# Tokenizer loop: the token products with stationary and moving operand traded, two tokens side by side in the array, and two elementwise products on GpSimd

## What is computed

```
Ct = B[None] * C / (1.0 - dtA / 2) * dt[:, None]      # C is x
dA = (1.0 + dtA / 2) / (1.0 - dtA / 2)
dA_log = jnp.log(dA)
V = jnp.exp(dA_log[:, :, None] * l)                   # l = 0 .. 511
K = 2.0 * jnp.einsum('chn,hnl->chl', Ct, V).real      # c: 16 elements, h: 256 tokens, n: 64 states
```

## Time and profile before

| | |
|---|---|
| three runs | 1660.93, 1664.78, 1665.66 us (median 1664.78) |
| the profiled execution | 1662.74 us, of which the span is 1661.0 us |
| TensorE, weight loads, VectorE, ScalarE, GpSimd busy | 89%, 59%, 77%, 60%, 35% of the span |
| TensorE's granted clock, mean | 0.906 of 2.4 GHz |
| loop of the tokens | first matmul at 80.23 us, last copy from PSUM over at 222.1 us |

### The profile page before, as it was taken

One profiled execution on the slowest core, in us unless ns is written; L12 is line 12 of the kernel. 1 busy time (PEld: TensorE's weight loads), 2 busy tenths in 40 slices (PEclk: granted clock), 3 DMA queues, 4 the chain that ended last, 5 costly groups with the idle time before them and its releaser, 6 DMA issues. The chain is left out here.

```text
span 1661.0 us, 31577 instructions
## 1 busy us (share of the span) xinstructions
PE 1473.0 (89%) x11710; PEld 986.5 (59%) x11710; DVE 1272.4 (77%) x2389; ACT 1002.0 (60%) x2539; POOL 580.4 (35%) x600
## 2 busy tenths in 40 slices
PE   2099967999999999999978888789999599999997
PEld 2099955677766777667756766567665244444443
DVE  8999926777777777777753346269998599999996
ACT  7799916887888877888752224178885233333331
POOL 0000004545445544454530000027777433333332
PEclk9555558999999999999988699989999899999998
DMA  2022252332333233332245037177785244444443
GB/s 83 1 51 64 61 151 84 100 101 94 104 125 102 94 95 105 116 103 98 94 161 178 0 116 241 47 217 206 214 221 137 52 103 101 101 101 102 102 102 83
DMA packets 233098, 183.09 MB, mean 110 GB/s; under 512 B 163568, under 2 KB 164976, under 8 KB 232944
## 3 DMA queue, kind: packets, MB, share of 16 engines
q1 hardware_dynamic: 232944, 181.07, 38.1%
HBM read 93.98 MB, written 59.77 MB: 93 GB/s over the span
## 5 line engine op out<-in xcount | busy, mean ns | idle before, releaser
L1063 PE MATMUL al_ps<-w,al_xT 128*128 128x512 f32 (+2 forms) x1024 | 351.3, 497 | 0.0
L1063 PEld LDWEIGHTS al_ps<-w,al_xT 128*128 128x128 f32 x1024 | 192.2, 193 | 127.1 <-issue 107.3
L2221 POOL TENSOR_TENSOR ff_zq<-ff_z,ff_back 128x1024 bf16<-128x1024 fp8e4 x64 | 122.6, 1915 | 222.9 <-DVE ff_z L2245 222.9
L451 PE MATMUL tk_ps<-tk_w,tk_l 128*128 128x64 f32 x512 | 119.6, 422 | 57.7 <-DVE tk_w L420 50.8
L2187 ACT ACTIVATE ff_sg<-af_ps 128x1024 f32<-128x1024 f32 x64 | 65.5, 1024 | 150.7 <-PE af_ps L2270 150.7
L451 PEld LDWEIGHTS tk_ps<-tk_w,tk_l 128*128 128x128 f32 x512 | 114.2, 332 | 60.3 <-issue 60.3
L756 POOL TENSOR_TENSOR al_qv<-al_qv,al_qe 128x512 f32<-128x512 f32 x48 | 63.2, 1316 | 219.8 <-PE al_ps L1126 219.8
L2270 PE MATMUL af_ps<-wgT,xqT 128*128 128x512 bf16 x512 | 122.7, 383 | 13.6 <-ACT ff_sg L2187 13.6
L2291 PE MATMUL af_ps<-wdT,ff_zT 128*128 128x512 bf16 x512 | 123.9, 386 | 5.9 <-DMA ff_zT<-ff_zq 5.9
L2270 PE MATMUL af_ps<-wuT,xqT 128*128 128x512 bf16 x512 | 122.1, 381 | 6.8 <-DVE ff_z L2237 4.8
L2042 PE MATMUL af_ps<-ag_w,ag_aT 128*128 128x512 f32 x256 | 112.6, 593 | 1.7 <-ACT af_ps L1878 1.7
(11 more groups left out here) (299 smaller groups left out, 3388.8 us busy)
## 6 DMA issues: line engine op xcount, KB each, us to landing
al_hx<-h_s SPq DMA_DIRECT2D x36, 256.0 KB, 2.7
o_s<-al_o SPq DMA_DIRECT2D x32, 272.0 KB, 2.2
h_s<-tk_w SPq DMA_DIRECT2D x16, 512.0 KB, 3.8
v_s<-al_v SPq DMA_DIRECT2D x32, 256.0 KB, 2.3
k_s<-al_kT SPq DMA_DIRECT2D x32, 256.0 KB, 2.3
q_s<-al_qT SPq DMA_DIRECT2D x32, 256.0 KB, 2.7
lt_k<-k_s SPq DMA_DIRECT2D x16, 512.0 KB, 5.0
lt_v<-v_s SPq DMA_DIRECT2D x16, 512.0 KB, 3.7
```

Of the source, the lines that this page charges most:

```text
L451: ins = pe.matmul(o, L[:, u, 0, t], R[:, u, t], start=True, stop=t < CS)
L1063: ins = pe.matmul(out, xT[:, T, k], w[:, k, cols], start=False, stop=True, skip_group_check=True)
L2221: pool.tensor_tensor(zq[:, u].rearrange("p (k s) -> p k s", s=QB), z8[:, u].rearrange("p (k s) -> p k s", s=QB), back[:, u, :, None].to_br ...
```

## The change

L is no longer summed: both k go to TensorE for all 16 tokens. The operands trade places. R(t), 64 columns, is now stationary, and L(k, t), 128 columns, moving. The 64 x 128 result of an even token goes to partitions 0 to 63 of PSUM and that of the odd one to 64 to 127, with the two alternating in program order. The result of a pair is a transposed one, so ScalarE copies it to `mid` (`turned`), TensorE transposes it (`turns`, 8 for a chunk, one chunk late), and ScalarE copies that to `hs` (`tokens`). R's product and the multiplication a · frequency go to GpSimd; ScalarE adds the offset in one instruction for the chunk.

```diff
@@ scalar
             def phases(ch):
-                if ch >= 2:
-                    act.wait_ge(nf_ready, ch - 1)
-                for t in range(CH):
-                    ins = act.activation(ph[:, ch % 2, t], c("iota_a"), ACT.Identity,
-                                         scale=par[:, 1, ch * CH + t:ch * CH + t + 1], bias=c("off_r"))
-                ins.then_inc(ph_ready, 1)
+                act.wait_ge(raw_ready, ch + 1)
+                act.activation(ph[:, ch % 2], ph[:, ch % 2], ACT.Identity, bias=c("off_r")).then_inc(ph_ready, 1)
...
+            def turned(ch):
+                act.wait_ge(mm_ready, ch + 1)
+                if ch >= 2:
+                    act.wait_ge(tr_ready, ch - 1)
+                for k in range(2):
+                    ins = act.activation(mid[:, ch % 2, 4 * k:4 * k + 4], ps[ch % 2 * 2 + k][:].rearrange(
+                        "p (j q) -> p j q", j=4), ACT.Copy)
+                ins.then_inc(mid_ready, 1)
+
             def tokens(ch):
-                act.wait_ge(mm_ready, ch + 1)
+                act.wait_ge(tr_ready, ch + 1)
...
                 if ch:
-                    tokens(ch - 1)
+                    turned(ch - 1)
+                if ch >= 2:
+                    tokens(ch - 2)
+            tokens(NCH - 2)
+            turned(NCH - 1)
             tokens(NCH - 1)
+
+        @block.gpsimd
+        def _(pool):
+            def raw(ch):
+                if ch >= 2:
+                    pool.wait_ge(nf_ready, ch - 1)
+                t0 = ch * CH
+                pool.tensor_tensor(ph[:, ch % 2], par[:, 1, t0:t0 + CH, None].to_broadcast([P, CH, 64]),
+                                   c("iota_a")[:, None, :].to_broadcast([P, CH, 64]), ALU.mult).then_inc(raw_ready, 1)
+
+            pool.wait_ge(s_ld, 80)
+            pool.wait_ge(s_xd, 4)
+            pool.wait_ge(s_par, 2)
+            raw(0)
+            pool.wait_ge(s_pb, 1)
+            for ch in range(NCH):
+                t0, u = ch * CH, ch % 2
+                if ch + 1 < NCH:
+                    raw(ch + 1)
+                pool.wait_ge(sin_ready, ch + 1)
+                pool.wait_ge(s_er, ch // 2 + 1)
+                if ch >= 2:
+                    pool.wait_ge(mm_ready, ch - 1)
+                pool.tensor_tensor(R[:, u], nf[:, u], ER[:, t0:t0 + CH], ALU.mult).then_inc(r_ready, 1)
@@ vector
                 for k in range(2):
-                    ins = dve.tensor_tensor(L[:, u, k] ...
-                    st.mark(ins)
-                st.wait(st.n)
-                dve.tensor_tensor(L[:, u, 0, 0:CS], L[:, u, 0, 0:CS], L[:, u, 1, 0:CS], ALU.add).then_inc(l_ready, 1)
-                dve.wait_ge(sin_ready, ch + 1)
-                dve.wait_ge(s_er, ch // 2 + 1)
-                dve.tensor_tensor(R[:, u], nf[:, u], ER[:, t0:t0 + CH], ALU.mult).then_inc(r_ready, 1)
+                    dve.tensor_tensor(L[:, u, k] ... ALU.mult).then_inc(l_ready, 1)
                 if ch + 1 < NCH:
                     fractions(ch + 1)
@@ tensor
+            def turns(ch):
+                pe.wait_ge(mid_ready, ch + 1)
+                if ch >= 2:
+                    pe.wait_ge(hs_ready, ch - 1)
+                for j in range(PAIRS):
+                    ins = pe.transpose(ps[4 + ch % 2 * 2 + j // 4][:, (j % 4) * P:(j % 4) * P + P],
+                                       mid[:, ch % 2, j], ident)
+                ins.then_inc(tr_ready, 1)
...
-                for t in range(CH):
-                    o = ps[u * 2 + t // 8][:, (t % 8) * 64:(t % 8) * 64 + 64]
-                    ins = pe.matmul(o, L[:, u, 0, t], R[:, u, t], start=True, stop=t < CS)
-                    if t >= CS:
-                        ins = pe.matmul(o, L[:, u, 1, t], R[:, u, t], start=False, stop=True)
+                for j in range(PAIRS):
+                    for k in range(2):
+                        for half in range(2):
+                            t = 2 * j + half
+                            ins = pe.matmul(ps[u * 2 + j // 4][64 * half:64 * half + 64, (j % 4) * P:(j % 4) * P + P],
+                                            R[:, u, t], L[:, u, k, t], start=k == 0, stop=k == 1)
                 ins.then_inc(mm_ready, 1)
+                if ch:
+                    turns(ch - 1)
+            turns(NCH - 1)
```

More of the change, by code:

```diff
@@ L120, in tokenizer @@
     CH = 16
-    CS = 13
+    PAIRS = CH // 2
     NCH = TOK // CH
@@ L151, in tokenizer @@
                  for k in range(2))
+        mid = nat[:, 0:16].rearrange("p k a n -> p (k a n)").rearrange("p (u j q) -> p u j q", u=2, j=PAIRS)
         ps = [ctx.enter_context(nc.psum_tensor(f"tk_ps{i}", [P, 512], F32)) for i in range(8)]
@@ L179, in tokenizer @@
         s_pb = sem("tk_pbd")
+        raw_ready = sem("tk_raw_ready")
+        mid_ready = sem("tk_mid_ready")
+        tr_ready = sem("tk_tr_ready")
         ph_ready = sem("tk_ph_ready")
@@ L270, in tokens @@
                 for k in range(2):
-                    ins = act.activation(hs[:, ch % 2, 8 * k:8 * k + 8], ps[ch % 2 * 2 + k][:].rearrange(
+                    ins = act.activation(hs[:, ch % 2, 8 * k:8 * k + 8], ps[4 + ch % 2 * 2 + k][:].rearrange(
                         "p (t a) -> p t a", t=8), ACT.Copy)
                 ins.then_inc(hs_ready, 1)
-            act.wait_ge(s_xd, 4)
-            act.wait_ge(s_par, 2)
             phases(0)
@@ L411, in _ @@
                 for k in range(2):
-                    ins = dve.tensor_tensor(L[:, u, k].rearrange("p t (c b) -> p t c b", b=8),
-                                            X[:, k, t0:t0 + CH, :, None].to_broadcast([P, CH, BATCH, 8]),
-                                            Pb[:, k, t0:t0 + CH, None, :].to_broadcast([P, CH, BATCH, 8]), ALU.mult)
-                    st.mark(ins)
-                st.wait(st.n)
-                dve.tensor_tensor(L[:, u, 0, 0:CS], L[:, u, 0, 0:CS], L[:, u, 1, 0:CS], ALU.add).then_inc(l_ready, 1)
-                dve.wait_ge(sin_ready, ch + 1)
-                dve.wait_ge(s_er, ch // 2 + 1)
-                dve.tensor_tensor(R[:, u], nf[:, u], ER[:, t0:t0 + CH], ALU.mult).then_inc(r_ready, 1)
+                    dve.tensor_tensor(L[:, u, k].rearrange("p t (c b) -> p t c b", b=8),
+                                      X[:, k, t0:t0 + CH, :, None].to_broadcast([P, CH, BATCH, 8]),
+                                      Pb[:, k, t0:t0 + CH, None, :].to_broadcast([P, CH, BATCH, 8]), ALU.mult
+                                      ).then_inc(l_ready, 1)
                 if ch + 1 < NCH:
@@ L442, in _ @@
             pe.wait_ge(s_ev, 16)
+            def turns(ch):
[6 more added lines that the diff above has]
+                ins.then_inc(tr_ready, 1)
             for ch in range(NCH):
                 u = ch % 2
-                pe.wait_ge(l_ready, ch + 1)
+                if ch >= 2:
+                    pe.wait_ge(mid_ready, ch - 1)
                 pe.wait_ge(r_ready, ch + 1)
-                if ch >= 2:
-                    pe.wait_ge(hs_ready, ch - 1)
-                for t in range(CH):
-                    o = ps[u * 2 + t // 8][:, (t % 8) * 64:(t % 8) * 64 + 64]
-                    ins = pe.matmul(o, L[:, u, 0, t], R[:, u, t], start=True, stop=t < CS)
-                    if t >= CS:
-                        ins = pe.matmul(o, L[:, u, 1, t], R[:, u, t], start=False, stop=True)
+                pe.wait_ge(l_ready, 2 * ch + 2)
+                for j in range(PAIRS):
[4 more added lines that the diff above has]
+                                            R[:, u, t], L[:, u, k, t], start=k == 0, stop=k == 1)
                 ins.then_inc(mm_ready, 1)
+                if ch:
+                    turns(ch - 1)
+            turns(NCH - 1)
 def three_parts(nc, dve, st, row, parts, tmp):
```

## The result

The changed kernel takes 1671.7 us (median of ten runs, 1668.16 to 1678.94) where the kernel before takes 1666.16 in ten runs; the ratio is 1.0039, with a 95% interval of 1.0023 to 1.0055. It is slower by some 5.5 us; 12.8 were forecast, and a median of 1678. The profiled execution has a span of 1666.3 us.

A forecast was written before the change was run, and what follows sets the result against it. VectorE set the pace, with ScalarE and TensorE all but full; afterwards VectorE and GpSimd taking turns would. +1.8, +0.7, +8.3 and +2 gave +12.8 on 1662.74, 1675.5; with 2.0 for the median, 1678 us, range 1672 to 1690.

The forecast's parts named there:

- GpSimd and VectorE exclude each other: In the loop, VectorE's two-SBUF-input instructions and GpSimd's products take turns, so a chunk takes the sum of the five.
- A chunk's length: In the loop, five products taking turns: 9.5 us a chunk, with 9.4 and 10.1 as the ends, for 8.83 before.
- The rule word for word: The skill's rule that the second waits for the whole instruction: full lengths, 10.1 us a chunk, a time near 1688.
- The loop: 15 chunks at 9.5 us less 1.8: 140.7 for 132.4 us, +8.3 (+6.8 to +17.2).
- Ahead of the loop: Before the loop, the first a · frequency product pushes busy VectorE by one turn: +1.8 us (0 to 1.9).
- First chunk: From `s_pb` to the first matmul: 9.5 for 8.8 us, +0.7 (0.6 to 1.3).
- The end: After the last chunk's first matmul: 9.0 us at full clock, 14.1 at lower, for 9.5; -0.5 to +4.6, taken +2.
- The stages behind the loop: After the loop nothing should change but its start; the sum held no term for it.
- 33 slots: TensorE's 64 records a chunk, halves overlapping, one 128-column slot per two records: 7.0 us at lower clock, 3.5 at full.
- No exclusion (1616): Rival: long products don't exclude each other, 5.8 us a chunk with TensorE at full clock, 1616 us; chance 0.10.
- VectorE keeping the port: Rival: GpSimd gets in only when VectorE runs dry, some 11.2 us a chunk, 1704 us; chance 0.08.
- the range of 1669 to 1700: Whole kernel: nearly all of the forecast, the same-time rival in part and the third's mild part; chance 0.8.

The follow-up runs named there:

- two other mixes: Changed kernel with R back on VectorE: 1656.34 us; kernel before with only the two products on GpSimd and the offset in one ScalarE instruction: 1705.36 us.
- the GpSimd part alone: Kernel before with only the two products on GpSimd and the offset in one ScalarE instruction, L's sum and TensorE's part unchanged: 1705.36 us, ratio 1.0234.
- the last version: Version with X in PSUM, a · frequency of chunk c+2 ahead of R(c), first two chunks' phases by small ScalarE instructions: 1614.66 us, ratio 0.9696.

## Why the prediction was right

By its own steps:

- **GpSimd and VectorE exclude each other.** Right, and now shown for long instructions: each of the four lines has records that are longer by the other's turn, in the order that I wrote down (fractions, L0, R, L1, a · frequency), and reading X from PSUM frees L's products from it. The Trainium skill's page "SBUF — State Buffer", section "Who interferes with whom", gives the condition (two SBUF inputs of VectorE against a reading GpSimd instruction), and the runs agree with it: 6.65 us for the pair with two SBUF inputs, 4.47 with one.
- **A chunk's length.** Measured 9.42. The turns counted by the earlier trace rows gave 9.4, and I took 9.5 with 0.1 for semaphores, of which 9.42 leaves hardly anything. The rule word for word, with full lengths, gave 10.1: an instruction that waited ends 0.13 to 0.16 us sooner than its length alone. The same arithmetic gave 8.4 and 11.2 for two other mixes, measured 8.39 and 11.22.
- **The loop**, +8.3 forecast: measured 222.41 - 82.89 = 139.5 for 132.4, +7.1. The last distance is 7.70, a chunk less the absent a · frequency.
- **Ahead of the loop**, +1.8: measured 73.25 for 71.39, +1.9. L409 took 2.00 us behind GpSimd's first product. **First chunk**, +0.7: measured 9.64 for 8.84, +0.8.
- **The end**, +2 as the middle between two clocks: measured 231.5 - 222.4 = 9.1 for 9.5, -0.4. TensorE was at its full clock (3.71 us for the products), so the low end held. Of the stage's terms this one was off most.
- These add up to +9.4 for the stage, 3.4 under my 12.8. **The stages behind the loop** were taken to keep their time. They did not: they gave 4.1 us back, 1.7 of it in the last product alone, where TensorE met its other clock. That is the missing term. It is no gain that the change brings as such: in the GpSimd part alone the stage ended 38.8 us later and the span 42.9, so there the same stages lost 4.1 us. The sum should have carried a term for it, zero in the middle and some 5 us to either side.
- **TensorE.** 33 slots: 3.5 us at the full clock, measured 3.71 for records with their last end. The halves overlap with 128 moving columns: 109 ns for two records, where a column takes 0.84 ns and one record alone would fill 107. The row that I took this from was weaker than I read it: 34 columns at 0.84 ns are 29 ns, all of L1155's 29 ns a record, so it showed loads that overlap and no moving columns that do. That its clock would not matter in the loop was right, since it waited for L in every chunk.
- **The rivals.** No exclusion (1616) is refuted by the records. VectorE keeping the port is refuted by R, which is done between the two products of L although both are queued.
- **Where the number landed.** The measured 1671.7 is the low end of the sum's own range (1672), and +5.5 us lies just above the +5 that I had given 0.03 of 0.76. The mechanism and the 9.4 us a chunk are no luck. That the total still fell into the range of 1669 to 1700 owes something to the width of that range: of the 7.5 us too many (12.8 for the profiled executions' 5.3), 3.4 were in the stage and 4.1 behind it, both to the same side.

Open: why the clock of TensorE falls differently in later stages when a stage ahead of them ends some microseconds earlier or later. The rows show that it does, not by what. Open too: what makes VectorE's TENSOR_SCALAR instructions wait with one SBUF input (below).

## What to carry to other kernels

Before a product is moved from VectorE to GpSimd, look at what stays on VectorE: if those instructions read two tensors of SBUF, and GpSimd's reads SBUF too, the move adds GpSimd's longer time to theirs instead of hiding it, and three engines can fall idle without a gain. Put one operand into PSUM, and place GpSimd's work beside those instructions; here that turned a loss of 0.4% into a gain of 3.0%. What was freed is a TENSOR_TENSOR with one operand in PSUM and one in SBUF. One SBUF input is not enough by itself: L409, a TENSOR_SCALAR that reads one tensor of SBUF, took 2.00 us beside GpSimd's first product and ended 0.14 us behind it, where its twin before took 0.28, and L946 and L962, which read one tensor too, have long cases. A busy time that rises while the work falls is a wait inside the records; compare the minimum and the median of a line to see it. Where weight loads of 128 columns stand against 64 moving ones, trading the operands onto two halves of the array halves the time of the products at the same clock (two records every 213 ns for one), before the transposes that it asks for.

## What the runs showed of the hardware

- An instruction that waits for the other engine's turn then takes less than its length alone: R ended 2.2 us after L0 (2.39 with X in PSUM, where it did not wait), a · frequency 1.8 after L1 (1.91), the fractions 1.1 after that (1.21).
- GpSimd and VectorE took turns in every chunk of the changed kernel, even where the next instruction of the same engine was already queued.
- Two halves of the array start two fp32 records of 128 moving columns every 109 ns at a granted clock of 1.00 and every 213 ns at 0.50 (the changed kernel's first chunk). At 1.00 the order of the records within eight did not matter.
- TensorE at 80.00 busy of 80 us stayed at a granted clock of 0.50 over the whole loop with 128 stationary and 64 moving columns; with the operands traded, and idle for 0.8 to 0.9 us in each chunk, it was granted 0.99 (the last version, 90 to 170 us).
- A TENSOR_SCALAR of VectorE with one SBUF input waited for GpSimd's product too: L409 took 2.00 us, and its twin in the kernel before, with GpSimd idle, 0.28:

```profile
22.66 0.28 DVE L371 TENSOR_SCALAR tk_c<-tk_par 128x256 f32<-128x256 f32 x1
```
